# A mixture-of-experts kernel with expert tiles of 128 rows instead of 256, and two sets of first-layer sum banks

## The chip, the cores and the metric

The kernel runs on one core of a Trainium2 chip. The metric is the device time of one execution in microseconds (us). TensorE (PE in the rows) multiplies matrices, and its weight loads are listed apart (PEld); VectorE is DVE, ScalarE is ACT, GpSimd is POOL, and SyncE (SP) issues DMA transfers. Each engine has an instruction queue of its own, whose register and semaphore instructions are listed as PEldq, DVEq, ACTq, POOLq and SPq.

## The reference, cut to what matters

4096 tokens (64 items of 64 rows, 256 features) pass through an adapter layer with a layer norm, a second norm with a style, and then a mixture of 8 experts in which each token uses its best two:

```python
probs = jax.nn.softmax(h_flat @ router_w, axis=-1)
gates, idx = jax.lax.top_k(probs, 2)
gates = gates / gates.sum(-1, keepdims=True)
...
hid = jax.nn.relu(jnp.einsum('nd,edf->nef', h_flat, exp_w1) + exp_b1)   # D = 256, FF = 1024
eout = jnp.einsum('nef,efd->ned', hid, exp_w2) + exp_b2
y = jnp.einsum('ned,ne->nd', eout, combine)
return x + y.reshape(x.shape)
```

The kernel computes only the two chosen experts of each token, so 8192 rows in all.

## The kernel before

The program has two stages. `dense` computes everything up to the router. It also splits the expert weights into two f16 parts (`w_high`, `w_low`) that stay on the chip, and scatters each token's row twice, into the queues in memory of its two experts; `fill_queues` puts `SLOTS` rows of padding behind each queue. A table then says for each of `TILES` expert tiles which expert it belongs to and where its rows begin. It is computed on VectorE at L1018 to L1036, while GpSimd scatters the last rows. `TILES` is fixed at the most that 8192 rows can need with 8 experts, so all tiles are always run, the last ones perhaps on padding.

`experts` then takes tile after tile, each with `SLOTS` = 256 rows, 39 tiles. The work on one tile i:

- SyncE reads the tile's place and loads its rows (L1104) into one of two buffers. It waits until tile i-2 is transposed and until VectorE has taken what it needs of tile i-2's row fields (`meta_taken`, given at L1267).
- TensorE transposes the rows (L1143), VectorE copies the transposed rows to `rT` (L1249).
- First layer (`layer_in`, L1165): for each of 8 blocks c of 128 hidden features, 6 matmuls sum into one half of a bank. The weights are the stationary operand, the tile's rows the one that streams: 48 matmuls of 256 columns. The place of the weights depends on the expert, which is in a register of TensorE's queue (read at L1152).
- ScalarE applies bias and relu from the bank into `hid` (L1209), VectorE splits `hid` into two f16 parts, two blocks (512 columns) at a time (L1256, L1258).
- Second layer (`layer_out`, L1181): for each block of 128 rows (`SUB` = 2 of them), 24 matmuls of 256 columns, with the rows' hidden features as the stationary operand.
- VectorE scales and adds the bias to `yb` (L1287, once for each 128 rows) and computes the gates in eight small steps (L1266 to L1280). ScalarE multiplies by the gate (L1224), and GpSimd adds 128 rows at a time to the output with an indirect DMA (L1122). Each of these waits until the one before it has landed.

The order on each engine is written out. On TensorE it is, in the loop: first layer of tile i, transposes of tile i+1, second layer of tile i-1. On VectorE it is: splits of i, copy to `rT` of i+1, `yb` of i-1, gates of i. The loop of each engine holds two tiles (i even and odd); its branch is at L1192 on TensorE. The first layer's sums use banks 0 to 3, and block c of a tile waits until ScalarE has read the same block of the tile before. Waits go through two helpers, at L82 and L88.

Of the kernel before, what the change touches and what calls it, by code (L numbers as in the profile page):

```python
# [27 lines left out]
F16 = mybir.dt.float16  # L28
# [3 lines left out]
ACT = mybir.ActivationFunctionType  # L32
# [3 lines left out]
ITEMS, T, D = 64, 64, 256  # L36
A, ADAPTERS = 64, 16
SUBJECTS, SE, SH = 32, 64, 128
EXPERTS, FF = 8, 1024
# [4 lines left out]
GROUPS = TOKENS // GROUP  # L44
GT = GROUP // P
GI = GROUP // T
SUB = 2
SLOTS = SUB * P
TILES = (2 * TOKENS + EXPERTS * (SLOTS - 1)) // SLOTS
QUEUE = TOKENS + SLOTS  # L50
# [28 lines left out]
def wait(eng, sem, value):  # L79

    if not isinstance(value, int) or value > 0:
        eng.wait_ge(sem, value)  # L82
# [56 lines left out]
def dense(nc, sem, env):  # L139
# [10 lines left out]
    with ExitStack() as ctx:  # L150
# [103 lines left out]


        G = TILES * EXPERTS
        assert 3 * G + 2 * TILES + 8 * 16 + TOKENS // SLOTS * EXPERTS <= 2 * GT * D
        tabs = rb[:, :, :, :].rearrange("p a t d -> p (a t d)")

        def grid(k):  # L260
# [6 lines left out]
            at = 3 * G + 2 * TILES + k * EXPERTS  # L267
            return tabs[:, at:at + EXPERTS]

        over = tabs[:, 3 * G + 2 * TILES + 8 * 16:3 * G + 2 * TILES + 8 * 16 + TOKENS // SLOTS * EXPERTS]  # L270
        def float_field(rows, at):
            return rows[:, :, at:at + 2].bitcast(F32).rearrange("p t o -> p (t o)")

# [765 lines left out]
def experts(nc, sem, env):  # L1039
# [5 lines left out]
    with ExitStack() as ctx:  # L1045
# [25 lines left out]
                             "gated", "added"))  # L1071


        PAIRS = FC // 2

        def ps_in(c):
            return banks[:, c // 2, (c % 2) * SLOTS:(c % 2 + 1) * SLOTS]

        def ps_rT(par):
            return banks[:, 4 + par, :].bitcast(F16)  # L1080

        def ps_out(par):
            return banks[:, 6 + par, :].rearrange("p (s d) -> p s d", d=D)

        def part_of(par, s, k, c):

# [9 lines left out]
        with nc.Block() as block:  # L1096
# [37 lines left out]
            @block.tensor  # L1134
            def _(pe):
                def transpose_rows(i):
                    pe.wait_ge(rows_loaded[i.par], (i.half + 1) * 16)
                    wait(pe, rT_ready, i.g - 1)
                    for k in range(2):
                        for c in range(DC):  # L1140
                            for s in range(SUB):
                                at = (k * DC + c) * SLOTS + s * P
                                last = nc.tensor.transpose(ps_rT(i.par)[:, at:at + P],  # L1143
                                                           part_of(i.par, s, k, c), ident16[:])
                    last.then_inc(rT_done, 1)

                held = [pe.alloc_register("even_expert"), pe.alloc_register("odd_expert")]

                def expert(i, load=False):

                    if load:
                        pe.reg_load(held[i.par], tile_expert[0:1, bass.ds(i.g, 1)])  # L1152
                    return pe.snap(held[i.par], min_val=0, max_val=EXPERTS - 1)

                def layer_in(i):
                    e = expert(i, load=True)
                    pe.wait_ge(rT_ready, i.g + 1)
                    for c in range(FC):
                        if c % 2 == 0:
                            wait(pe, hid_ready, (i.g - 1) * PAIRS + c // 2 + 1)  # L1160
                        n = 0
                        for k in range(DC):
                            at = bass.ds(e * (DC * FF) + (k * FF + c * P), P)
                            for w, v in ((w_high, 0), (w_high, 1), (w_low, 0)):
                                last = nc.tensor.matmul(ps_in(c), w[:, at], rT[:, i.par, v, k, :],  # L1165
                                                        start=(n == 0), stop=(n == 3 * DC - 1))
                                n += 1
                        if c % 2 == 1:
                            last.then_inc(in_done, 1)

                def layer_out(i):
                    e = expert(i)
                    wait(pe, y_ready, i.g - 1)
                    for s in range(SUB):
                        n = 0
                        for c in range(FC):
                            if s == 0 and c % 2 == 0:
                                pe.wait_ge(split_low, i.g * PAIRS + c // 2 + 1)
                            at = bass.ds(e * (FC * D) + (W2_AT + c * D), D)
                            for w, v in ((w_high, hid_high), (w_high, hid_low), (w_low, hid_high)):  # L1180
                                last = nc.tensor.matmul(ps_out(i.par)[:, s, :], v[:, i.par, c, s * P:(s + 1) * P],  # L1181
                                                        w[:, at], start=(n == 0), stop=(n == 3 * FC - 1))
                                n += 1
                    last.then_inc(out_done, 1)

                transpose_rows(At(0, 0))
                layer_in(At(0, 0))
                transpose_rows(At(0, 1))
                layer_in(At(0, 1))
                transpose_rows(At(1, 0))  # L1190
                layer_out(At(0, 0))
                with pe.Fori(1, TILES // 2) as h:  # L1192
                    for c in (0, 1):
                        layer_in(At(h, c))
                        transpose_rows(At(h, c + 1))
                        layer_out(At(h, c - 1))
                layer_in(At(TILES // 2, 0))
                layer_out(At(TILES // 2, -1))
                layer_out(At(TILES // 2, 0))

            @block.scalar
            def _(sc):
                def bias_relu(i):
                    e = expert_of(sc, i)
                    for c in range(FC):
                        if c % 2 == 0:
                            sc.wait_ge(in_done, i.g * PAIRS + c // 2 + 1)
                            wait(sc, split_low, (i.g - 1) * PAIRS + c // 2 + 1)
                        last = nc.scalar.activation(hid[:, c, :], ps_in(c), ACT.Relu,  # L1209
                                                    scale=1.0 / WSCALE, bias=feat[:, bass.ds(e * FC + (B1 + c), 1)])  # L1210
                        if c % 2 == 1:
                            last.then_inc(hid_ready, 1)

                def choice_ratio(i):
                    sc.wait_ge(rows_loaded[i.par], (i.half + 1) * 16)
                    wait(sc, gate_ready, i.g)
                    nc.scalar.activation(ratio[:], field(i.par, ROW_DIFF, F32), ACT.Exp).then_inc(ratio_ready, 1)  # L1217

                def times_gate(i):
                    sc.wait_ge(y_ready, i.g + 1)  # L1220
                    sc.wait_ge(gate_ready, i.g + 1)
                    wait(sc, added, (i.g - 1) * SUB * 16)
                    for s in range(SUB):
                        nc.scalar.activation(yg[:, i.par, s, :], yb[:, s, :], ACT.Copy,  # L1224
                                             scale=gate[:, i.par, s:s + 1]).then_inc(gated, 1)

                bias_relu(At(0, 0))
                choice_ratio(At(0, 0))
                bias_relu(At(0, 1))
                choice_ratio(At(0, 1))  # L1230
                times_gate(At(0, 0))
                with sc.Fori(1, TILES // 2) as h:
                    for c in (0, 1):
                        bias_relu(At(h, c))
                        choice_ratio(At(h, c))
                        times_gate(At(h, c - 1))
                bias_relu(At(TILES // 2, 0))
                choice_ratio(At(TILES // 2, 0))
                times_gate(At(TILES // 2, -1))
                times_gate(At(TILES // 2, 0))  # L1240

            @block.vector
            def _(dve):
                V = nc.vector

                def rows_out(i):
                    dve.wait_ge(rT_done, i.g + 1)
                    wait(dve, in_done, (i.g - 1) * PAIRS)
                    V.tensor_copy(rT[:, i.par].rearrange("p k c s -> p (k c s)"), ps_rT(i.par)).then_inc(rT_ready, 1)  # L1249

                def split(i, pair):
                    n = i.g * PAIRS + pair + 1
                    dve.wait_ge(hid_ready, n)
                    wait(dve, out_done, i.g - 1)
                    s = slice(pair * 2, pair * 2 + 2)
                    V.tensor_copy(hid_high[:, i.par, s, :], hid[:, s, :]).then_inc(split_high, 1)  # L1256
                    dve.wait_ge(split_high, n)
                    V.tensor_tensor(hid_low[:, i.par, s, :], hid[:, s, :], hid_high[:, i.par, s, :],  # L1258
                                    ALU.subtract).then_inc(split_low, 1)
# [29 lines left out]
                    last.then_inc(y_ready, 1)  # L1289

                def splits(i):
                    for pair in range(PAIRS):
                        split(i, pair)

                rows_out(At(0, 0))
                splits(At(0, 0))
# [70 lines left out]
```

## Time and profile before

| | us |
|---|---|
| runs | 709.71, 711.25, 716.42 |
| median of the runs | 711.25 |
| profiled execution, span from first to last instruction | 709.8 |
| TensorE busy | 587.4 (83% of the span) |
| VectorE busy | 445.1 (63%) |
| ScalarE busy | 284.0 (40%) |
| GpSimd busy | 257.7 (36%) |

The busy times are means over both stages. The dense stage fills the span up to about 250 us, the expert stage the rest. The profile prints for the span in 40 slices how busy each engine is, in tenths; TensorE stands at 9 in every slice of the expert stage but its first ones, while its granted clock is full. In the dense stage TensorE, VectorE and ScalarE change places as the busiest. The profiled execution's own device time is not listed apart from its span.

### The profile page before, as it was taken

To read this page: it belongs to the slowest core of one execution; us is meant where nothing else is said; L and a number is where in the kernel's file an instruction comes from. 1 tells how busy PE (TensorE), PEld (TensorE's weight loads), DVE (VectorE), ACT (ScalarE), POOL (GpSimd) and SP (SyncE) were. 2 spreads that over 40 slices of the span, in tenths; PEclk is the share of its full clock that TensorE was granted. 3 is DMA by queue.
4 is the path that set the end of the run, shared out by engine and by line. 5 is a ranking of instruction groups with operands and counts; after the bars stand their busy time and mean duration, and the time that the engine had idled before them with its cause. 6 is when DMAs were issued, how large, how long until landed. Compare 5 with 4: busy or idle time off the path is not lost.

```text
span 709.8 us, 17109 instructions
## 1 busy us (share of the span) xinstructions
PE 587.4 (83%) x4832; PEld 508.1 (72%) x4833; DVE 445.1 (63%) x1456; ACT 284.0 (40%) x631; POOL 257.7 (36%) x215
## 2 busy tenths in 40 slices
PE   0977876888643048999999999999999999999990
PEld 0754664666632037989989989899899898998980
DVE  3358988788786424655656656567566665565650
ACT  0328755466544022433433424334334343343420
POOL 3002386667787400322323223322232233222322
PEclk9759878777755568999999999999999999999995
DMA  4245645334543520323322323332233233332322
GB/s 168 66 148 182 210 146 206 110 130 149 201 129 133 188 89 17 54 52 45 52 43 48 58 37 52 52 45 52 40 54 55 37 52 52 45 52 42 50 28 22
DMA packets 42971, 60.20 MB, mean 85 GB/s; under 512 B 4852, under 2 KB 36085, under 8 KB 42805
## 3 DMA queue, kind: packets, MB, share of 16 engines
q1 hardware_dynamic: 27558, 40.13, 17.8%
q0 software_dynamic: 14304, 18.75, 16.0%
q10 hardware_dynamic: 1088, 1.07, 0.5%
q8 instruction: 10, 0.16, 0.1%
q14 instruction: 11, 0.09, 0.0%
HBM read 33.41 MB, written 25.46 MB: 83 GB/s over the span
## 4 chain that ended last, share of the span: by engine, by line
PE 60%; DMA 2%; issue 1%; DVE 1%; ACT 0%; POOL 0%; SPq 0%; POOLq 0%; ACTq 0%; DVEq 0%
PE banks L1165 29%; PE banks L1181 28%; PE banks L1143 2%; DMA out<-yg,token 2%; DMA rows<-queues 0%; POOL out L1122 0%; DVE rT L1249 0%; ACT L1217 0%; DVE hid_low L1258 0%; ACT hid L1209 0%; ACT yg L1224 0%; DVE yb L1287 0%; SPq L1101 0%; DVE hid_high L1256 0%; ACT ratio L1217 0%
## 5 line engine op out<-in xcount | busy, mean ns | idle before, releaser
L1122 POOL DMA_INDIRECT out<-yg,token x78 | 126.3, 1620 | 333.6 <-ACT yg L1224 208.6
L1165 PE MATMUL banks<-rT,w_high 128*128 128x256 f16 x1248 | 210.8, 276 | 5.0 <-DVE rT L1249 5.0
L1165 PE MATMUL banks<-rT,w_low 128*128 128x256 f16 x624 | 172.0, 276 | 0.0
L1181 PE MATMUL banks<-w_high,hid_low 128*128 x624 | 170.1, 273 | 0.0
L1181 PE MATMUL banks<-w_high,hid_high 128*128 x624 | 170.1, 273 | 0.0
L1181 PE MATMUL banks<-w_low,hid_high 128*128 x624 | 170.1, 273 | 0.0
L1209 ACT ACTIVATE hid<-banks,feat 128x256 f32<-128x256 f32 x312 | 127.1, 472 | 74.7 <-PE banks L1165 67.5
L1165 PEld LDWEIGHTS banks<-rT,w_high 128*128 x1248 | 123.4, 99 | 20.9 <-issue 5.5
L1224 ACT ACTIVATE yg<-yb,gate 128x256 f32<-128x256 f32 x78 | 35.4, 500 | 220.5 <-DVE yb L1287 220.5
L1258 DVE TENSOR_TENSOR hid_low<-hid,hid_high 128x512 f16<-128x512 f32 x156 | 108.4, 695 | 5.3
L1287 DVE SCALAR_TENSOR_TENSOR yb<-banks,b 128x256 f32<-128x256 f32 x78 | 29.5, 420 | 114.3 <-PE banks L1181 114.3
L1256 DVE CAST hid_high<-hid 128x512 f16<-128x512 f32 x156 | 72.2, 463 | 42.6 <-ACT hid L1209 42.5
L469 POOL DMA_INDIRECT queues<-h_rows,slot x64 | 73.1, 1142 | 22.5 <-issue 18.6
L1165 PEld LDWEIGHTS banks<-rT,w_low 128*128 x624 | 61.9, 99 | 7.8
L1181 PEld LDWEIGHTS banks<-w_low,hid_high 128*128 128x128 f16 x624 | 61.1, 98 | 7.0
L1181 PEld LDWEIGHTS banks<-w_high,hid_low 128*128 128x128 f16 x624 | 61.1, 98 | 6.7
L1181 PEld LDWEIGHTS banks<-w_high,hid_high 128*128 128x128 f16 x624 | 61.1, 98 | 6.6
L579 PE MATMUL banks<-rw,hT 128*128 128x8 f32 x128 | 25.5, 337 | 35.9 <-ACT hT L672 35.9
L579 PEld LDWEIGHTS banks<-rw,hT 128*128 128x128 f32 x128 | 24.8, 297 | 38.7 <-ACT hT L672 38.7
L1143 PE MATMUL banks<-ident,rows 128*128 128x128 f16 x312 | 24.2, 221 | 22.2 <-DMA rows<-queues 22.2
L885 DVE SCALAR_TENSOR_TENSOR w_low<-stage,w_high 128x1024 f16<-128x1024 f32 (+1 forms) x32 | 37.3, 1219 | 1.1 <-issue 0.6
L1143 PEld LDWEIGHTS banks<-ident,rows 128*128 128x128 f16 x312 | 20.9, 99 | 23.2 <-DMA rows<-queues 22.3
(167 smaller groups left out, 680.1 us busy)
## 6 DMA issues: line engine op xcount, KB each, us to landing
stage<-expert_w SPq DMA_DIRECT2D x32, 512.0 KB
rows<-queues SPq DMA_DIRECT2D x39, 260.0 KB
xb<-x SPq DMA_DIRECT2D x8, 512.0 KB
out<-rb SPq DMA_DIRECT2D x8, 512.0 KB, 3.2
queues<-pad_row SPq DMA_DIRECT2D x5, 260.0 KB
out<-yg,token POOLq DMA_INDIRECT x78, 3.8
queues<-pad_row ACTq DMA_DIRECT2D x4, 260.0 KB
wnow<-w_low SPq DMA_DIRECT2D x8, 128.0 KB, 3.2
```

Source lines behind the costliest of these rows:

```text
L469: nc.gpsimd.indirect_dma_start(out=queues, out_offset=bass.IndirectOffsetOnAxis(ap=slot[:, i.par, t, k:k + 1], axis=0), in_=h_rows[:, i.pa ...
L579: last = nc.tensor.matmul(ps_lg[:, t, :], hT[:, c, t * P:(t + 1) * P], rw[:, c, :], start=(c == 0), stop=(c == DC - 1))
L885: V.scalar_tensor_tensor(w_low[:, w], stage[:, slot], WSCALE, w_high[:, w], ALU.mult, ALU.subtract).then_inc(w_low_ready, 1)
L1122: nc.gpsimd.indirect_dma_start(out=out, out_offset=bass.IndirectOffsetOnAxis(ap=token[:, i.par, s:s + 1], axis=0), in_=yg[:, i.par, s, :], ...
L1143: last = nc.tensor.transpose(ps_rT(i.par)[:, at:at + P], part_of(i.par, s, k, c), ident16[:])
L1165: last = nc.tensor.matmul(ps_in(c), w[:, at], rT[:, i.par, v, k, :], start=(n == 0), stop=(n == 3 * DC - 1))
L1181: last = nc.tensor.matmul(ps_out(i.par)[:, s, :], v[:, i.par, c, s * P:(s + 1) * P], w[:, at], start=(n == 0), stop=(n == 3 * FC - 1))
L1209: last = nc.scalar.activation(hid[:, c, :], ps_in(c), ACT.Relu, scale=1.0 / WSCALE, bias=feat[:, bass.ds(e * FC + (B1 + c), 1)])
L1224: nc.scalar.activation(yg[:, i.par, s, :], yb[:, s, :], ACT.Copy, scale=gate[:, i.par, s:s + 1]).then_inc(gated, 1)
L1256: V.tensor_copy(hid_high[:, i.par, s, :], hid[:, s, :]).then_inc(split_high, 1)
L1258: V.tensor_tensor(hid_low[:, i.par, s, :], hid[:, s, :], hid_high[:, i.par, s, :], ALU.subtract).then_inc(split_low, 1)
L1287: last = V.scalar_tensor_tensor(yb[:, s, :], ps_out(i.par)[:, s, :], 1.0 / WSCALE, b2[:, bass.ds(e * D, D)], ALU.mult, ALU.add)
```

## The change

The tile has 128 rows (`SUB` = 1), so there are 71 tiles. A first-layer matmul streams 128 columns instead of 256; a bank of 512 columns holds four blocks of features (`QUAD`) instead of two, so a tile's sums need two banks instead of four, and even and odd tiles use different pairs. Block c now waits for ScalarE's reading of tile i-2 instead of i-1. Semaphores count per bank of four blocks. The split is still over 512 columns. The second layer's matmuls keep 128 by 256. One table moves to another buffer, since it grew.

```diff
-SUB = 2
+SUB = 1
 SLOTS = SUB * P
 TILES = (2 * TOKENS + EXPERTS * (SLOTS - 1)) // SLOTS
...
-        over = tabs[:, 3 * G + 2 * TILES + 8 * 16:3 * G + 2 * TILES + 8 * 16 + TOKENS // SLOTS * EXPERTS]
+        over = nb[:, :, :].rearrange("p t d -> p (t d)")[:, 0:TOKENS // SLOTS * EXPERTS]
...
-        PAIRS = FC // 2
-
-        def ps_in(c):
-            return banks[:, c // 2, (c % 2) * SLOTS:(c % 2 + 1) * SLOTS]
+        QUAD = 512 // SLOTS
+        QUADS = FC // QUAD
+
+        def ps_in(par, c):
+            return banks[:, par * QUADS + c // QUAD, (c % QUAD) * SLOTS:(c % QUAD + 1) * SLOTS]
...
                     for c in range(FC):
-                        if c % 2 == 0:
-                            wait(pe, hid_ready, (i.g - 1) * PAIRS + c // 2 + 1)
+                        if c % QUAD == 0:
+                            wait(pe, hid_ready, (i.g - 2) * QUADS + c // QUAD + 1)
                         n = 0
                         for k in range(DC):
                             at = bass.ds(e * (DC * FF) + (k * FF + c * P), P)
                             for w, v in ((w_high, 0), (w_high, 1), (w_low, 0)):
-                                last = nc.tensor.matmul(ps_in(c), w[:, at], rT[:, i.par, v, k, :],
+                                last = nc.tensor.matmul(ps_in(i.par, c), w[:, at], rT[:, i.par, v, k, :],
                                                         start=(n == 0), stop=(n == 3 * DC - 1))
                                 n += 1
-                        if c % 2 == 1:
+                        if c % QUAD == QUAD - 1:
                             last.then_inc(in_done, 1)
...
-                            if s == 0 and c % 2 == 0:
-                                pe.wait_ge(split_low, i.g * PAIRS + c // 2 + 1)
+                            if s == 0 and c % QUAD == 0:
+                                pe.wait_ge(split_low, i.g * QUADS + c // QUAD + 1)
...
-                    s = slice(pair * 2, pair * 2 + 2)
+                    s = slice(quad * QUAD, (quad + 1) * QUAD)
```

The waits of ScalarE and VectorE change in the same way, from two blocks to four.

## Rows read from the trace of the kernel before

**Rows 1.** Busy time in a stretch: us, PE, PEld, DVE, ACT, POOL, clock, DMA.
```profile
400.00:500.00 100.00, 100.00 (x953) 90.05 (x952) 61.62 (x171) 38.20 (x99) 30.08 (x19) 1.00 0.30 49
```

**Rows 2.** Groups of instructions, 300 to 710 us: busy, mean ns, idle before.
```profile
L1165 PE MATMUL banks<-rT,w_high 128*128 128x256 f16 x1120 | 185.3, 273 | 0.0
...
L1249 DVE COPY rT<-banks 128x1024 f16<-128x1024 f16 x35 | 23.9, 681 | 0.0
```

**Rows 3.** Waits, 300 to 710 us: who waited for whom, total, times, longest.
```profile
DVE yb L1287 <- PE banks L1181: 108.2, 37, 3.2
```

**Rows 4.** The chain of waits (first row), then TensorE in order of time.
```profile
435.17 5.24 PE banks L1165 x48
...
505.80 0.61 PE L1143 MATMUL banks<-ident,rows 128*128 128x128 f16 x8
506.25 0.27 PE L1181 MATMUL banks<-w_high,hid_high 128*128 x1
```

**Rows 5.** TensorE in order of time, first and last expert matmuls.
```profile
256.70 0.60 PE L1165 MATMUL banks<-rT,w_high 128*128 128x256 f16 x2 [0.88 <-DVE rT L1249]
...
691.00 0.27 PE L1181 MATMUL banks<-w_low,hid_high 128*128 x1
```

**Rows 6.** TensorE's queue at L1165 (starts, first to last), and TensorE's own start.
```profile
L1165 PEldq FUSED_REGOPS  x16: 46/46/52, 303.0 to 307.0; - x16
...
303.88 0.38 PE L1165 MATMUL banks<-rT,w_high 128*128 128x256 f16 x2
...
L1165 PEldq FUSED_REGOPS  x8: 46/46/51, 256.6 to 258.3; - x8
```

**Rows 7.** TensorE's queue after the first layer of the same tile, by line.
```profile
L1137 PEldq FUSED_REGOPS  x1: 42/42/42, 307.2 to 307.2; - x1
...
L1153 PEldq FUSED_REGOPS  x1: 41/41/41, 308.2 to 308.2; - x1
...
L1181 PEldq FUSED_REGOPS  x8: 46/46/60, 308.4 to 310.2; - x8
```

**Rows 8.** Load of a tile's rows and the bias step before, in order of time.
```profile
305.46 0.38 SPq L1104 DMA_DIRECT2D rows<-queues  x1
...
304.29 0.76 DVE L1287 SCALAR_TENSOR_TENSOR yb<-banks,b 128x256 f32<-128x256 f32 x2 [3.16 <-PE banks L1181]
```

**Rows 9.** TensorE's queue at the head of two tiles, by line.
```profile
L1192 PEldq ALU_OP  x1: 32/32/32, 301.9 to 301.9; - x1
...
L1152 PEldq FUSED_REGOPS  x1: 42/42/42, 312.9 to 312.9; - x1
...
L1165 PEldq FUSED_REGOPS  x2: 46/46/46, 313.8 to 314.0; - x2
```

**Rows 10.** ScalarE in order of time; a group of ScalarE's, 300 to 710 us.
```profile
328.30 1.57 ACT L1209 ACTIVATE hid<-banks,feat 128x256 f32<-128x256 f32 x4 [0.37 <-issue]
330.04 0.47 ACT L1209 ACTIVATE hid<-banks,feat 128x256 f32<-128x256 f32 x1 [0.17 <-PE banks L1165]
...
L1217 ACT ACTIVATE ratio<-rows 128x2 f32<-128x2 f32 x35 | 7.1, 203 | 0.0
```

**Rows 11.** VectorE in order of time, two splits.
```profile
307.45 0.43 DVE L1256 CAST hid_high<-hid 128x512 f16<-128x512 f32 x1 [1.15 <-ACT hid L1209]
307.91 0.69 DVE L1258 TENSOR_TENSOR hid_low<-hid,hid_high 128x512 f16<-128x512 f32 x1
308.52 0.42 DVE L1256 CAST hid_high<-hid 128x512 f16<-128x512 f32 x1
```

**Rows 12.** GpSimd in order of time, the last two additions.
```profile
697.23 1.56 POOL L1122 DMA_INDIRECT out<-yg,token  x1 [3.01 <-DMA out<-yg,token]
701.58 1.56 POOL L1122 DMA_INDIRECT out<-yg,token  x1 [2.79 <-DMA out<-yg,token]
```

**Rows 13.** End of the dense stage in order of time, VectorE and GpSimd.
```profile
238.35 0.17 DVE L1036 TENSOR_SCALAR tile_row<-rb 1x39 int32<-1x39 f32 x1
...
242.20 0.96 POOL L469 DMA_INDIRECT queues<-h_rows,slot  x1 [0.30 <-issue]
```

**Rows 14.** Busy time in two stretches of the dense stage, columns as in rows 1.
```profile
60.00:80.00 20.00, 15.07 (x82) 10.69 (x80) 17.55 (x66) 15.19 (x26) 7.79 (x8) 0.98 0.57 194
190.00:210.00 20.00, 6.45 (x38) 6.29 (x37) 17.30 (x69) 10.85 (x20) 15.70 (x13) 0.59 0.35 120
```

More of the change, by code:

```diff
@@ L256, in dense @@
         G = TILES * EXPERTS
-        assert 3 * G + 2 * TILES + 8 * 16 + TOKENS // SLOTS * EXPERTS <= 2 * GT * D
+        assert 3 * G + 2 * TILES + 8 * 16 <= 2 * GT * D and TOKENS // SLOTS * EXPERTS <= GT * D
         tabs = rb[:, :, :, :].rearrange("p a t d -> p (a t d)")
@@ L1071, in experts @@
                              "gated", "added"))
-        PAIRS = FC // 2
-        def ps_in(c):
-            return banks[:, c // 2, (c % 2) * SLOTS:(c % 2 + 1) * SLOTS]
+        QUAD = 512 // SLOTS
+        QUADS = FC // QUAD
+        def ps_in(par, c):
+            return banks[:, par * QUADS + c // QUAD, (c % QUAD) * SLOTS:(c % QUAD + 1) * SLOTS]
         def ps_rT(par):
-            return banks[:, 4 + par, :].bitcast(F16)
+            return banks[:, 4 + par, 0:2 * DC * SLOTS // 2].bitcast(F16)
         def ps_out(par):
-            return banks[:, 6 + par, :].rearrange("p (s d) -> p s d", d=D)
+            return banks[:, 6 + par, 0:SUB * D].rearrange("p (s d) -> p s d", d=D)
         def part_of(par, s, k, c):
@@ L1205, in bias_relu @@
                     for c in range(FC):
[L1206 to L1209, printed above, removed]
+                        if c % QUAD == 0:
+                            sc.wait_ge(in_done, i.g * QUADS + c // QUAD + 1)
+                            wait(sc, split_low, (i.g - 1) * QUADS + c // QUAD + 1)
+                        last = nc.scalar.activation(hid[:, c, :], ps_in(i.par, c), ACT.Relu,
                                                     scale=1.0 / WSCALE, bias=feat[:, bass.ds(e * FC + (B1 + c), 1)])
-                        if c % 2 == 1:
+                        if c % QUAD == QUAD - 1:
                             last.then_inc(hid_ready, 1)
@@ L1247, in rows_out, with split @@
                     dve.wait_ge(rT_done, i.g + 1)
-                    wait(dve, in_done, (i.g - 1) * PAIRS)
+                    wait(dve, in_done, (i.g - 1) * QUADS)
                     V.tensor_copy(rT[:, i.par].rearrange("p k c s -> p (k c s)"), ps_rT(i.par)).then_inc(rT_ready, 1)
-                def split(i, pair):
-                    n = i.g * PAIRS + pair + 1
+                def split(i, quad):
+                    n = i.g * QUADS + quad + 1
                     dve.wait_ge(hid_ready, n)
                     wait(dve, out_done, i.g - 1)
-                    s = slice(pair * 2, pair * 2 + 2)
+                    s = slice(quad * QUAD, (quad + 1) * QUAD)
                     V.tensor_copy(hid_high[:, i.par, s, :], hid[:, s, :]).then_inc(split_high, 1)
@@ L1291, in splits @@
                 def splits(i):
-                    for pair in range(PAIRS):
-                        split(i, pair)
+                    for quad in range(QUADS):
+                        split(i, quad)
                 rows_out(At(0, 0))
```

## The prediction

> **What bounds the kernel now.** I read the slices of the span first, which show the expert stage as the long even stretch at the end, and then the table of stretches inside it: of 100 us there TensorE is busy all 100, clock 1.00, VectorE 62, ScalarE 38, GpSimd 30 [rows 1]. The groups of that stage show matmuls that stream 256 columns, with no idle time before them [rows 2]; the waits name VectorE, ScalarE and GpSimd as those who wait, never TensorE [rows 3]. So one tile costs what TensorE takes for it. In the chain of waits 48 matmuls of a layer take 5.24 us, 0.109 us each, and in order of time the 8 transposes of 128 columns take 0.45 us from the first start to the start of the next matmul, 0.056 us each [rows 4]. A tile of 256 rows is 96 x 0.109 + 8 x 0.056 = 10.92 us, and 39 tiles are 426 us. TensorE's first expert matmul starts at 256.7 and the last ends near 691.3 [rows 5], 434.6 us, so 8 us are start-up, the rest is this product.
>
> **What TensorE would need after.** First layer: 48 matmuls of 128 columns; second layer: 24 of 256 columns; 4 transposes. At the starts just read: 48 x 0.056 + 24 x 0.109 + 4 x 0.056 = 2.69 + 2.62 + 0.22 = 5.53 us per tile, 71 tiles 393 us, 33 us less than now, since 71 x 128 is 9% fewer rows than 39 x 256. This is the gain if the array stays the bound.
>
> **What feeds TensorE.** The same 48 first-layer pairs (weight load, matmul) per tile must be handed out by TensorE's instruction queue, whatever their width. The weights are addressed with the expert's register, so each group of three pairs carries two register instructions at L1165, one fused and one plain. The records of the queue itself show its pace: in a tile that TensorE only begins at 303.88, the queue starts the 16 groups between 303.0 and 307.0 [rows 6]. With the last group's own time that is 4.2 us for work that takes the array 5.24, so the queue runs ahead of the array and this is its free pace. At the first tile, with the queue nearly empty and the array at the low clock, eight groups start between 256.6 and 258.3 [rows 6], 1.7 / 7 = 0.24 us per group. The array can't have paced it: two matmuls took it 0.60 us there [rows 5]. So a group of three costs the queue 0.24 us. With 256 columns the array needs 0.327 and hides it; with 128 columns it needs 0.168 and cannot. In the second layer nothing changes: 0.327 against 0.24.
>
> Against it stands the reading of the transposes, 0.056 us per pair [rows 4]: a row that says that narrow pairs run at the array's pace. But they have no register instruction among them and were waiting in the queue.
>
> The Trainium skill (TensorE: Matmul & The Clock Gate, Back-to-back issue gap) gives both: an isolated gap of about 56 ns at 128 columns, and about 81 ns for a sustained stream of weight load and matmul pairs. The trace has 0.056 us and 0.24 / 3 = 0.080 us for the two. By the first the first layer would take 2.7 us per tile, by the second 3.9.
>
> **The queue's time for one tile after**, each piece from records in which it isn't held:
> - first layer: 16 x 0.24 = 3.84; the whole run is 4.2 now with three waits inside, so about 0.1 each, and one wait is left inside: 3.9 to 4.0. I take 4.0.
> - two waits and 4 transposes: from L1137 at 307.2 to L1153 at 308.2 [rows 7] the queue now stands a microsecond, but that is for the tile's rows, whose load was issued at 305.46 [rows 8]. Free, 0.2 to 0.3: 0.25.
> - L1153 at 308.2 to L1181 at 308.4: 0.2. Second layer: eight groups from 308.4 to 310.2 [rows 7] and the last group's 0.2, 2.0. (The 24 pairs of the second half tile, which follow to 312.9 while the queue is full, go.)
> - the next tile's head: branch and expert number, 301.9 to 303.0 in one tile of the loop, 312.9 to 313.8 in the other [rows 9]: 1.0 on average.
>
> Sum 4.0 + 0.25 + 0.2 + 2.0 + 1.0 = **7.45 us per tile** against 5.53 of the array. 71 x 7.45 = 529 us against 426: +103. Bounds: 7.1 if the waits and transposes are nearly free, 7.9 if a wait adds to it; that is 504 to 561.
>
> **What lies beside it at 7.45.** From the first group's start as zero: the first layer's last sum is there at 4.3. ScalarE now does 256 columns every 0.366 us (four in 1.57, one 0.47) and 2 columns in 0.20 [rows 10], so about 0.24 for 128; its last four end at 5.5. VectorE's split stays 512 wide, 0.43 and 0.69, one pair each 1.07 us [rows 11], ending at 6.6; the copy into rT at L1249 halves (0.68 now, 0.4 then [rows 2]), ending near 7.05, and the queue asks for it at about 7.35. Only 0.3 is spare: if it is late, all of the difference comes on the tile. The two sets of sum banks remove the wait for ScalarE from the tile before, which costs nothing now [rows 3] and wouldn't have been late either. The rows of tile i+2 are asked for after the first gate instructions, now 1.17 us after yb starts, with two bias steps [rows 8]; one bias step is 0.34 less. Their landing takes at most 2.75 from issue with 256 rows, 305.46 to 308.2 [rows 7, 8]; issued near 8.5, landed by 11.2, wanted at 7.45 + 4.0 = 11.5. Covered, barely. The adds to the output: one starts 4.35 us after the one before when chained, 4.6 at most in other places [rows 12]; there is now one per tile, 4.6 of 7.45, and 71 instead of 78. VectorE per tile: 2.1 + 0.4 + 0.4 + 1.4 for the eight gate steps, 4.3; below.
>
> **Ends.** Grid tables of 71 instead of 39 tiles lengthen about six VectorE instructions by 0.4 each (8 columns a tile) at L1024 to L1034, and they end by 238.5, under GpSimd's scatters, which run to 243.2 [rows 13]: nothing. The nine pad fills halve, too, beside the same scatters: nothing, 2 us at most. Start-up: 8 us now, half of it the low clock on full-width matmuls, which the queue's pace covers: -3. Tail: now the last TensorE work ends at 691.3 and four adds queue behind each other, the last at 701.58 [rows 12], and the span ends 18.5 us after TensorE; with one add per tile only two are left, the last starting 3.75 after TensorE's end and 8.2 of landing and closing behind it (701.58 to 709.8): 12.0. -6.5. Sum: 709.8 + 103 - 3 - 6.5 = 803.3. The span is 1.45 under the median of the runs, so **805**.
>
> **Rivals.**
> *The queue doesn't bind (not slower).* If register instructions and pairs are handed out at the array's pace once it is hungry, as the transposes' 0.056 suggests, the array's 5.53 holds: 709.8 - 33 - 9.5 = 667. It decides below 0.168 us per group. Against it: 0.24 and, waits taken off, 0.24 again in the two tiles of rows 6. 5%. It is also what the isolated gap of the Trainium skill (same page and section) would give.
> *The row load binds.* Without the queue's bound a cycle closes: end of second layer, yb and gate steps with the issue 0.85, landing 2.1 (the load halves) to 2.75, transposes 0.25, second layer 2.62, and 0.4 of wake-ups: 6.2 to 6.9 us, 71 x gives 440 to 490, in all 716 to 765. It is under 7.45, so it shows only if the queue is faster than I read: 8%.
> *The clock falls.* The array would work 5.5 of 7.45 us in short bursts. Earlier stages show clocks of 0.59 at a TensorE busy share of 0.32 and 0.98 at 0.75 [rows 14]; 0.74 is like the second, though what counts as busy is unclear. At the low level a tile needs twice 5.3, about 10.7; one tile in three at it gives (2 x 7.45 + 10.7) / 3 = 8.5, in all 880, one in ten 830. 10%.
> *Waits add.* If the copy to rT or the rows come 0.3 to 0.6 late each tile: 825 to 850. 10%.
> My forecast, queue-bound at 7.1 to 7.7: 67%, 780 to 822.
>
> **Numbers.** Repeats of this kernel spread by 1%, so within 1% counts as no change. Faster: the array-bound case and a little of the load case, 6%. Same: the low end of the load case, 4%. Slower: 90%. The range 765 to 860 holds the forecast, the waits and the mild part of the clock case; the array-bound case, most of the load case and the rest of the clock case, 5 + 7 + 7%, lie outside.
>
> **What will show it.** TensorE busy share down from all to about three quarters in the expert stage, its idle time ascribed to issue and not to VectorE or DMA; at L1165 the 16 groups still 3.8 to 4.1 us long, now with matmuls starting in threes every 0.24; tiles 7.45 apart in the row loads; a clock of 1.00. If tiles are 5.5 to 6.9 apart, the queue's price was wrong; if matmuls start 0.107 apart, the clock fell; if TensorE waits on rT or rows by name, the slack was.

## The result, and the profile after

The changed kernel takes 788.47 us in the median of four runs (788.15 to 789.4), the kernel before 710.48 beside it; the ratio is 1.110, with a 95% interval of 1.105 to 1.115. The profiled execution spans 786.6 us. The forecast was 805, slower, in a range of 765 to 860.

The table of stretches in the expert stage, columns as in [rows 1]:

```profile
400.00:500.00 100.00, 97.62 (x1045) 75.37 (x1044) 55.47 (x195) 39.14 (x135) 21.84 (x14) 1.00 0.22 36
```

The clock is full. TensorE still seems busy, 97.6 of 100, but that is an effect of overlapping records: a narrow matmul's record is 0.22 us long, and the next one starts inside it. The weight loads have shorter records, 0.10 us each, and show more of the gaps: 90 us of 100 were filled before (the same table has 90.05 for PEld in [rows 1]), 75 are now. The groups from 300 to 770 us name what the loads waited for:

```profile
L1166 PEld LDWEIGHTS banks<-rT,w_high 128*128 x2072 | 117.8, 97 | 81.2 <-issue 24.9
```

Of the 81.2 us of idle time before these loads the profile ascribes 24.9, all to "issue", time in which nothing that the profile shows was waited for; the rest it ascribes to nothing. TensorE in order of time inside one first layer shows the rhythm (a row with x2 holds two matmuls):

```profile
504.96 0.28 PE L1166 MATMUL banks<-rT,w_high 128*128 128x128 f16 x2
505.08 0.22 PE L1166 MATMUL banks<-rT,w_low 128*128 128x128 f16 x1
505.19 0.28 PE L1166 MATMUL banks<-rT,w_high 128*128 128x128 f16 x2
```

Three pairs take 0.23 us here; over whole layers in the stage it is 0.24 to 0.25. They don't come evenly: two matmuls start within 0.12 us, 0.06 each, and from the third to the first of the next group it is another 0.11. The chain of work that ended last, in order of time, gives the tile; its columns are start, length and what:

```profile
500.00 0.38 PE banks L1144 x4
500.39 2.75 PE banks L1182 x24
503.13 0.32 issue
503.45 4.12 PE banks L1166 x48
507.57 0.00 issue
507.58 0.38 PE banks L1144 x4
507.96 2.73 PE banks L1182 x24
510.70 3.89 PE banks L1166 x48
```

48 narrow first-layer pairs take 3.9 to 4.1 us, against 5.24 for 48 wide ones in [rows 4]. Half the columns, but three quarters of the time. From the transposes at 500.00 to those at 507.58 is one tile, 7.58; the next one takes 7.04 (514.62 is the next set of transposes), 7.30 on average over the stage's row loads, where it was 10.93. 71 x 7.30 = 518 us against 426.

TensorE's queue by line, one row for each piece of a tile, answers to [rows 6, 7, 9]:

```profile
L1193 PEldq ALU_OP  x1: 32/32/32, 502.3 to 502.3; - x1
L1166 PEldq FUSED_REGOPS  x16: 46/46/52, 503.3 to 507.1; - x16
L1138 PEldq FUSED_REGOPS  x1: 42/42/42, 507.4 to 507.4; - x1
L1154 PEldq MOVE  x1: 29/29/29, 507.6 to 507.6; - x1
L1182 PEldq FUSED_REGOPS  x8: 46/46/60, 507.8 to 509.6; - x8
L1153 PEldq FUSED_REGOPS  x1: 42/42/42, 509.8 to 509.8; - x1
L1166 PEldq FUSED_REGOPS  x3: 46/46/46, 510.5 to 511.0; - x3
```

The queue never stands: each piece begins where the last one ends. At L1138 it passes in 0.2 us where it stood for 1.0 in [rows 7]. The 16 groups of the first layer start between 503.3 and 507.1, about as before (303.0 to 307.0), and now TensorE does them in the same 4 us.

VectorE's copy to rT and the two additions that end the kernel, in order of time:

```profile
510.03 0.42 DVE L1250 COPY rT<-banks 128x512 f16<-128x512 f16 x1
...
774.63 1.56 POOL L1123 DMA_INDIRECT out<-yg,token  x1 [5.28 <-ACT yg L1225]
779.09 1.56 POOL L1123 DMA_INDIRECT out<-yg,token  x1 [2.90 <-DMA out<-yg,token]
```

The copy ends at 510.45, just as the queue comes to the first group at 510.5. It was given 0.3 us to spare, and over the stage that is the mean, but the two tiles of the loop share it unevenly. Behind the loop's branch the first group starts 0.54 us after the copy's end on average, in the other tile 0.04 to 0.07. In run 8 below, where the copy does hold the queue, 0.04 lies between the two. So in every second tile nothing is left. It costs hardly anything yet: in those tiles the queue takes 0.205 to 0.235 us from the expert's number to the first group, at most 0.03 over the shortest.

### The profile page after: what moved, and what is told of

It reads as the page before. It is cut to its first block, busy times and chain, and to the rows that moved or that the text cites. A ratio compares the mean times of both kernels' runs of the same rounds, so it can differ in the third digit from the quotient of the medians.

```text
span 786.6 us, 23620 instructions
## 1 busy us (share of the span) xinstructions
PE 656.1 (83%) x6172; PEld 508.3 (65%) x6173; DVE 467.7 (59%) x1709; ACT 322.3 (41%) x912; POOL 242.5 (31%) x208
## 4 chain that ended last, share of the span: by engine, by line
PE 64%; issue 2%; DMA 1%; ACT 0%; DVE 0%; POOL 0%; SPq 0%; ACTq 0%; POOLq 0%; DVEq 0%
PE banks L1166 36%; PE banks L1182 24%; PE banks L1144 3%; DMA out<-yg,token 0%; DMA rows<-queues 0%; POOL out L1123 0%; ACT L1218 0%; DVE rT L1250 0%; ACT hid L1210 0%; ACT yg L1225 0%; SPq L1102 0%; DVE yb L1288 0%; ACT ratio L1218 0%; DVE norm L1272 0%; DVE second L1274 0%
## 5 line engine op out<-in xcount | busy, mean ns | idle before, releaser
L1166 PE MATMUL banks<-rT,w_high 128*128 128x128 f16 x2272 | 283.6, 225 | 16.2 <-issue 10.8
L1166 PE MATMUL banks<-rT,w_low 128*128 128x128 f16 x1136 | 250.6, 221 | 0.0
L1123 POOL DMA_INDIRECT out<-yg,token x71 | 110.9, 1562 | 429.3 <-ACT yg L1225 420.2
L1210 ACT ACTIVATE hid<-banks,feat 128x128 f32<-128x128 f32 x568 | 162.2, 368 | 170.9 <-PE banks L1166 170.9
L1182 PE MATMUL banks<-w_high,hid_high 128*128 x568 | 155.4, 274 | 0.1
L1182 PE MATMUL banks<-w_high,hid_low 128*128 x568 | 154.8, 273 | 0.0
L1182 PE MATMUL banks<-w_low,hid_high 128*128 x568 | 154.8, 273 | 0.0
L1166 PEld LDWEIGHTS banks<-rT,w_low 128*128 x1136 | 110.1, 97 | 1.3
L1259 DVE TENSOR_TENSOR hid_low<-hid,hid_high 128x512 f16<-128x512 f32 x142 | 98.3, 692 | 4.9
L469 POOL DMA_INDIRECT queues<-h_rows,slot x64 | 73.2, 1144 | 22.4 <-issue 18.5
L1250 DVE COPY rT<-banks 128x512 f16<-128x512 f16 x71 | 29.7, 418 | 14.2 <-PE banks L1144 14.2
```

Source lines behind the costliest of these rows:

```text
L469: nc.gpsimd.indirect_dma_start(out=queues, out_offset=bass.IndirectOffsetOnAxis(ap=slot[:, i.par, t, k:k + 1], axis=0), in_=h_rows[:, i.pa ...
L1123: nc.gpsimd.indirect_dma_start(out=out, out_offset=bass.IndirectOffsetOnAxis(ap=token[:, i.par, s:s + 1], axis=0), in_=yg[:, i.par, s, :], ...
L1166: last = nc.tensor.matmul(ps_in(i.par, c), w[:, at], rT[:, i.par, v, k, :], start=(n == 0), stop=(n == 3 * DC - 1))
L1210: last = nc.scalar.activation(hid[:, c, :], ps_in(i.par, c), ACT.Relu, scale=1.0 / WSCALE, bias=feat[:, bass.ds(e * FC + (B1 + c), 1)])
```

## The experiments

Theory Q: TensorE's queue sets the tile, through the two register instructions of each first-layer group. Rival L: a narrow pair takes the array about 0.08 us whatever feeds it. Both give 3.9 us for the first layer as it stands. The uneven starts above speak against L, but only a run that takes the register instructions away can decide. The letters S, R, V, T and D, each explained where it is first used, stand for what else might take part. Each run was timed against the kernel before on the same chip (ratio and interval in brackets). Where weights are taken from a fixed place, the kernel leaves out the choice of the expert there and doesn't compute the right result: such runs measure a cause, they are no candidates. "A tile" is the mean distance of the row loads in the expert stage.

**1. First-layer weights at fixed places, in the changed kernel.**

```diff
-                            at = bass.ds(e * (DC * FF) + (k * FF + c * P), P)
+                            at = slice(k * FF + c * P, k * FF + (c + 1) * P)
```

> Changed kernel, but TensorE's first layer takes its weights at fixed places (expert 0), so its 32 register instructions per tile are gone; the choice of the expert in the first layer is left out. Theory Q (TensorE's queue, its register instructions, sets the tile): the queue's time for a tile falls from 7.30 us by about 16 x 0.2 to near 4.1, below the array's 5.53, so the array (5.53 per tile) or the cycle through the row load (6.2 to 6.9) binds: 661, or 709 to 758. Theory L (a pair of weight load and matmul with 128 columns takes the array about 0.08 us whatever feeds it): stays at 786.

712.46 us (1.0015, 0.9997 to 1.0032). 76 us went with the register instructions, and TensorE shows what a narrow pair costs it when it is fed:

```profile
502.76 0.28 PE L1166 MATMUL banks<-rT,w_high 128*128 128x128 f16 x2
502.87 0.22 PE L1166 MATMUL banks<-rT,w_low 128*128 128x128 f16 x1
502.93 0.28 PE L1166 MATMUL banks<-rT,w_high 128*128 128x128 f16 x2
```

Three pairs in 0.17, 0.056 us each, over the whole layer of 48. That rules out L. But the tile is 6.17 us, not 5.53. The waits from 400 to 650 us and the chain name the load of the rows:

```profile
PEld banks L1144 <- DMA rows<-queues: 15.8, 40, 0.6
```
```profile
501.15 0.18 DVE is_first L1268
501.54 2.04 DMA rows<-queues
503.62 0.40 PE banks L1144 x4
504.02 2.70 PE banks L1182 x24
```

This is the cycle that the prediction priced at 6.2 to 6.9; it came out at the bottom of that, with the load landing 2.04 us after its issue.

**2. Only half of the groups at fixed places** (those with k = 1, the second 128 of the 256 input features).

> Changed kernel with the weights' places fixed only for the second half of the features (k = 1): 8 of the 16 first-layer groups lose their two register instructions; the choice of the expert is left out there. Q: the queue needs 7.30 - 8 x 0.2 = 5.7 us a tile, so 5.7 to 6.3, 673 to 716, more than with all fixed or equal to it if the row load's cycle binds both. L: 786.

712.92 us (1.0029, 1.0011 to 1.0047), a tile of 6.18. The same as with all fixed, so the second bound holds both, within what was written.

**3. One set of sum banks.**

```diff
-            return banks[:, par * QUADS + c // QUAD, (c % QUAD) * SLOTS:(c % QUAD + 1) * SLOTS]
+            return banks[:, c // QUAD, (c % QUAD) * SLOTS:(c % QUAD + 1) * SLOTS]
...
-                            wait(pe, hid_ready, (i.g - 2) * QUADS + c // QUAD + 1)
+                            wait(pe, hid_ready, (i.g - 1) * QUADS + c // QUAD + 1)
```

> Changed kernel with one set of first-layer sum banks: block c waits for ScalarE's reading of the tile before, as in the kernel before. Q: ScalarE is done with a tile's sums near 5.5 of the 7.3 us, before the next tile begins, so no change: 785 to 790. Rival S (the two sets carry part of the result): the tile grows by what ScalarE is late, 0.2 us or more, 800 and up.

793.65 us (1.116, 1.113 to 1.119), 5 us or 0.7% above the changed kernel's 788.47, which was timed apart from it; the intervals of the two ratios overlap a little. That is between the two expectations. No wait of TensorE for ScalarE appears in its list of waits, and the tile is 7.34 instead of 7.30 us: 3 of the 5 us. The register instructions of the waits fall differently in the queue (the first layer's run is 4.00 instead of 3.96 us, the piece before it 0.07 longer, the second layer 0.08 shorter). So the banks as such carry nothing of the result; another 1.1 us is ahead of the tiles, whose first transposes begin at 251.87 instead of 250.73.

**4. Narrow pairs in the kernel before**, with the tile of 256 rows and no more register instructions.

```diff
+                        for s in range(SUB):
...
-                                last = nc.tensor.matmul(ps_in(c), w[:, at], rT[:, i.par, v, k, :],
+                                    last = nc.tensor.matmul(ps_in(c)[:, s * P:(s + 1) * P], w[:, at],
+                                                            rT[:, i.par, v, k, s * P:(s + 1) * P],
```

> Kernel before, tiles of 256 rows, but each first-layer matmul cut into two of 128 columns, so that the tile has 96 first-layer pairs; the second 128 rows use the addresses already in registers, so there are no more register instructions. Q: the queue needs 7.7 plus 48 more pairs at about 0.015 to 0.02, 8.5 to 8.7 us, still under the array; the array needs 96 x 0.056 instead of 48 x 0.109, 0.15 us more: 715 to 717. L: 96 x 0.080 = 7.7 us for the first layer, 13.4 a tile, 805.

715.8 us (1.0066, 1.0046 to 1.0087), inside Q's 715 to 717. Its chain has the 96 pairs:

```profile
502.59 5.36 PE banks L1166 x96
```

0.056 us each, in a kernel that computes everything. Here the pairs of the second 128 rows also take their weights from a place that a register holds, without a register instruction of their own. At the first tile, with the array at the low clock and the queue ahead of it, the queue's records at the first layer's line, 256.44 to 258.4 us, show what they cost it:

```profile
L1166 PEldq FUSED_REGOPS  x6: 46/46/51, 256.4 to 257.7; - x6
```

The six records are 1.22 us apart from first to last by their exact starts, five steps of 0.24 each, although nine pairs lie in two of them and three in the others. So it is the register instruction that costs, not the register in a weight load's address.

**5 to 8. The load cut in two.** The features go into a buffer that is free once the tile two before is transposed, only the four fields of a row wait for the gate steps.

```diff
                     wait(sp, rT_done, i.g - 1)
+                    sp.dma_start(rows[:, i.par].bitcast(U32),
+                                 queues[bass.ds(row, SLOTS), 0:D].rearrange("(s p) d -> p s d", p=P)
+                                 ).then_inc(rows_loaded[i.par], 16)
                     wait(sp, meta_taken, i.g - 1)
-                    sp.dma_start(rows[:, i.par].bitcast(U32), queues[bass.ds(row, SLOTS)].rearrange("(s p) d -> p s d", p=P)
-                                 ).then_inc(rows_loaded[i.par], 16)
+                    sp.dma_start(fields[:, i.par].bitcast(U32),
+                                 queues[bass.ds(row, SLOTS), D:ROW // 2].rearrange("(s p) d -> p s d", p=P)
+                                 ).then_inc(fields_loaded[i.par], 16)
```

With all groups at fixed places:

> As the first experiment (first-layer weights at fixed places, choice of the expert left out there), and each tile's load cut in two: the features into a buffer that is free once the tile two before is transposed, the four fields of a row into one of their own that waits for the gate steps. Theory Q with the row load as second bound: the cycle that now sets 6.17 us a tile opens, the array's 5.53 to 5.6 is left: 711 - 71 x 0.6 = 668. Theory V (what holds that kernel at 6.17 is VectorE's order of splits, copy and bias, not the load): 711.

712.73 us (1.0016, 0.9992 to 1.0041), a tile of 6.18. A miss: I had taken the load as the only second bound. The waits from 400 to 650 us now name the other one:

```profile
PE banks L1172 <- DVE rT L1256: 19.7, 41, 0.6
```

In the changed kernel itself:

> Changed kernel, computing everything, with the load cut in two in the same way. Q: the queue sets 7.3 us a tile and the load is covered, no change: 785 to 790. Theory R (the row load takes part in the changed kernel's 7.3 us): faster by 0.2 us a tile or more, 772 or less.

790.53 us (1.111, 1.107 to 1.115), a tile of 7.30. The load takes no part in the changed kernel's time. (The half microsecond above what was expected lies ahead of the tiles: the first transposes begin 1.6 us later.)

With 4 and with 8 of the 16 groups at fixed places:

> Cut load, and 4 of the 16 first-layer groups at fixed places (choice of the expert left out in them). Q: each group without its two register instructions takes 0.2 us off the queue's 7.3: 6.5 us a tile, 786 - 57 = 730. Theory L (narrow pairs themselves): 786.

> Cut load, and 8 of the 16 groups at fixed places (choice of the expert left out in them). Q: 7.3 - 8 x 0.2 = 5.7 us a tile, a little over the array's 5.53: 672 to 680. Theory L: 786.

724.56 us (1.020, 1.016 to 1.024) and 713.03 us (1.0008, 0.9981 to 1.0035). The queue's register instructions at L1172 in one tile of each, the quarter first:

```profile
L1172 PEldq FUSED_REGOPS  x12: 46/46/46, 506.5 to 509.2; - x12
```
```profile
L1172 PEldq FUSED_REGOPS  x8: 46/46/46, 500.8 to 502.6; - x8
```

From the first register instruction of the layer to the wait behind it, means over the stage, 16 groups take 3.96 us (the changed kernel), 12 take 3.00, 8 take 2.03: each group taken away saves 0.24, and nothing is left for the 48 pairs. The quarter's tile is 6.34 us, 0.96 less than 7.30; it was expected at 6.5, with 0.2 for a group instead of 0.24. The half's queue would need 5.4 but its tile is 6.19, the same as with all fixed: the second miss, for the same reason.

**9 to 11. The copy to rT between the two splits.**

```diff
-                        splits(At(h, c))
-                        rows_out(At(h, c + 1))
+                        splits(At(h, c), At(h, c + 1))
```

where `splits` copies the next tile's rows after its first split. With all groups fixed and the load cut:

> First-layer weights at fixed places (choice of the expert left out there), load cut in two, and VectorE copies the next tile's transposed rows to rT between the two splits instead of behind them. Theory T (two cycles of nearly the same length stand under the queue: the row load, and first layer - bias and relu - split - copy to rT - next first layer, 6.17 us): with both open the array's 5.53 to 5.6 is left, 668 to 673. Theory D (one engine's own work or the additions set 6.17): 711.

682.66 us (0.958, 0.955 to 0.961), a tile of 5.75: theory T's direction, but 10 us above its range, the third miss. With 8 groups fixed:

> The same with only 8 of the 16 groups at fixed places. T and Q: the quarter gave 0.24 us a group, so the queue needs 7.30 - 8 x 0.24 = 5.4, or 5.7 by 0.2 a group: 668 to 680. D: 711.

683.19 us (0.959, 0.956 to 0.961), again 5.75, and 3 us above its range. With all fixed and the load in one piece:

> First-layer weights at fixed places (choice of the expert left out there) and the earlier copy to rT, but the load in one piece. T: the cycle through the row load alone still gives 6.1 to 6.2 us a tile: 706 to 713. If the copy to rT alone was the bound: 668.

711.77 us (1.0006, 0.9988 to 1.0023), 6.17 a tile. Its waits from 400 to 600 us name the load again:

```profile
PEld banks L1144 <- DMA rows<-queues: 12.5, 31, 0.6
```

So two cycles of the same 6.17 us lie under the queue's 7.30, and with the register instructions gone neither change alone gives anything. Together they give 0.42 us a tile. The array's 5.53 is not reached; TensorE's weight loads still wait for the copy to rT, between 400 and 600 us of run 9:

```profile
PEld banks L1172 <- DVE rT L1256: 7.8, 18, 0.5
```

The missing 0.22 us all lies in one place: from the start of a second layer's last matmul to that of the next first layer's first one it is 0.32 us on average in this run, where the kernel before, fed without a pause, has 0.11. The 7.8 us above would be 0.22 for each of the 35 tiles, but the same list puts another 4.0 down to issue, so that the copy is all of it is likely, not shown. What would have to move next wasn't tried, nor was the earlier copy in the changed kernel itself.

**12. Fixed places in the kernel before.**

> Kernel before with first-layer weights at fixed places (choice of the expert left out there), 32 register instructions per tile less. Q: its queue has over 3 us to spare in a tile of 10.93, so no change: 708 to 713. If register instructions cost the array time wherever they stand: 39 x 3.2 = 125 us less, 586.

710.53 us (0.998, 0.997 to 1.000). 32 register instructions less in a tile and no change: they cost only where the array is faster than the queue.

No kernel that computes everything came under the kernel before. The runs at 683 leave out the expert's choice in at least half of the first layer.

## Why the prediction was right, step by step

- **The bound before**, TensorE's columns: held. Narrow pairs alone moved it by the 0.12 us a tile that 96 pairs at 0.056 us give over 48 at 0.109 (run 4), and register instructions by nothing (run 12).
- **The array after**, 0.056 us a pair and 5.53 a tile: the pair's price was right in runs 1 and 4. In the changed kernel it is hidden.
- **The queue, 0.24 us a group**: right, and the cause. The removal of 4 groups' register instructions took 0.96 us from the tile; of all 16, as much as the next bound let go. The prediction gave the price to the group of three pairs as a whole; the runs show that all of it belongs to the two register instructions.
- **7.45 us a tile**: 7.30 measured. First layer 3.96 for 4.0, waits and transposes 0.23 for 0.25, the step to the second layer 0.19 for 0.2, second layer 2.04 for 2.0. The mis-sized term is the head, 1.0 in the sum and 0.88 measured: in rows as above, 502.3 to 503.3 in one tile, but 509.8 to 510.5 in the other, 0.7 where [rows 9] had 0.9. In all it is 0.15 a tile, 0.15 x 71 = 11 us of the 17 by which the span came out below 803.3.
- **The two sum sets cost and give nothing**: right to 0.04 us a tile.
- **The slack of what lies beside**: "only 0.3 is spare" for the copy, and the rows "covered, barely". Both named the right neighbours. The 0.3 holds only as a mean: the prediction took the head as 1.0 in both tiles of the loop, and the one with the shorter head has no slack at all. That the copy isn't late there is luck. The two cycles came out as 6.17 us each; the prediction had a price only for the load's (6.2 to 6.9) and none for the copy's, and the expectation of 668 for the first kernel with the cut load (run 5) failed on that.
- **Ends**: what TensorE needs from its first transposes to its last matmul beyond 71 or 39 mean tiles is 6.6 us instead of 10.3, -3.8 for -3. Tail 11.3 instead of 18.5, -7.3 for -6.5. The first transposes start at 250.73 instead of 254.80, 4.1 us sooner. Of that, 1.3 us lie between GpSimd's last scatter and the first transposes (239.47 to 250.73 against 242.20 to 254.80, 11.3 for 12.6; all kernels with 128-row tiles have 11.0 to 11.4, runs 4 and 12 with 256-row tiles 13.0 and 13.4). That fits the halved pad fills and loads, inside the "2 us at most", but no run took them apart. The other 2.7 is when the dense stage is done, which moves by as much between kernels whose dense stage is the same: in those with 128-row tiles its last scatter starts at 239.5 to 242.1.
- **The clock** stayed at 1.00 from 300 to 770 us; the rival that priced its fall did not come.
- **One sign was read off the wrong row**: the prediction looked for a busy share of TensorE of about three quarters. It is 97.6%, and the three quarters stand in the share of the weight loads.
- The rule that went with the forecast (the Trainium skill, TensorE: Matmul & The Clock Gate, Back-to-back issue gap) gives about 81 ns for a sustained pair at 128 columns. The changed kernel has 0.08 us a pair in its groups, but runs 1 and 4 sustain 0.056 over 48 and 96 pairs, so here the 0.08 is the register instructions' and not the pair's. That the two figures agree is a coincidence as far as these runs show.

## What to carry to other kernels

Halving what a matmul streams helps only as far as its queue can hand out the next one: count the register instructions between the pairs, and read their pace from the queue's own rows in a stretch where the queue runs ahead. Where one bound hides others, price every cycle below it before promising what its removal gives; here two of equal length stood there, and opening one alone gave nothing. A busy share of 97% was no sign of a full array, since the records of short matmuls overlap; their starts, one by one, show it.

## What the runs showed of the hardware that was not expected

A weight load and matmul pair without register instructions costs TensorE's queue next to nothing: taking the register instructions of 4 and of 8 groups away shortened the layer's run by 0.24 us for each group, the group's whole share, while the 48 pairs stayed (runs 7 and 8). In run 4 six more pairs in a step left it at 0.24 us. In the queue's records of the changed kernel the plain register instruction starts 0.124 us after the fused one (median), and the next fused one 0.113 us after it. So the price is about 0.12 us for each register instruction, 32 of them a first layer.
